# Row sums on ScalarE, other buffer bases, a reordered beginning, and a small matmul ahead of one product in each step

## What is computed

```
h   = x @ W0 + b0
x1  = layernorm(x + (adj @ h) / rowsum(adj))
u   = relu(adj @ (x1 @ W1) + b1)
u   = relu(adj @ (u  @ W2) + b2)
out = layernorm(x1 + adj @ (u @ W3) + b3)
```

## Time and profile before

| | us |
|---|---|
| median of 3 runs (lowest, highest) | 559.99 (559.52, 560.68) |
| the profiled execution | 559.2 |
| its span, first to last instruction | 557.3 |
| PE busy in the span | 545.2 (98%) |
| DVE, ACT, POOL busy | 352.3, 275.1, 207.3 |

### The profile page before, as it was taken

How to read it: one execution, slowest core, us unless ns; L and a number is a source line. 1 busy time by engine, 2 the same in 40 slices (tenths; PEclk the granted TensorE clock), 3 DMA queues, 4 the chain that set the end, 5 groups by cost and what they waited for, 6 DMA issues and landing times.

```text
span 557.3 us, 10510 instructions
## 1 busy us (share of the span) xinstructions
PE 545.2 (98%) x3664; PEld 499.7 (90%) x3664; DVE 352.3 (63%) x1075; ACT 275.1 (49%) x645; POOL 207.3 (37%) x224
## 2 busy tenths in 40 slices
PE   8899999999999999999999999999999999999996
PEld 8788989989899898989989899898989989899885
DVE  5764665747567475665747667475665756657455
ACT  5465454463644536454464644636454364543632
POOL 2647226081450906317071350905318072361000
PEclk9999999999999999999999999999999999999999
DMA  6900230503105050140503205040140502200002
GB/s 229 307 13 1 57 135 1 188 2 110 80 0 188 0 180 9 48 140 0 188 0 99 89 0 188 0 169 19 38 151 0 188 1 71 119 1 39 2 1 76
DMA packets 13270, 43.55 MB, mean 78 GB/s; under 512 B 1728, under 2 KB 2496, under 8 KB 13248
## 3 DMA queue, kind: packets, MB, share of 16 engines
q1 hardware_dynamic: 12960, 42.74, 22.4%
q10 hardware_dynamic: 288, 0.52, 0.3%
HBM read 34.87 MB, written 8.39 MB: 78 GB/s over the span
## 4 chain that ended last, share of the span: by engine, by line
PE 94%; issue 2%; DVE 2%; ACT 1%; DMA 1%; POOL 0%; POOLq 0%; DVEq 0%; SPq 0%
PE bank_a L157 16%; PE bank_a L159 16%; PE bank_a L158 16%; PE bank_b L157 15%; PE bank_b L158 15%; PE bank_b L159 15%; DMA adj_raw<-in_adjT 1%; DVE x_lo L555 0%; DVE x L604 0%; DVE v L597 0%; DVE h_lo L555 0%; POOL adj_lo L748 0%; ACT x_hi L459 0%; ACT adj_hi L396 0%; ACT bank_a L461 0%
## 5 line engine op out<-in xcount | busy, mean ns | idle before, releaser
L748 POOL TENSOR_TENSOR adj_lo<-adj_raw,adj_hi 128x512 fp32r<-128x512 f32 x61 | 77.0, 1295 | 288.3 <-ACT adj_hi L396 288.3
L555 DVE TENSOR_TENSOR x_lo<-bank_a,x_hi 128x512 fp32r<-128x512 f32 x64 | 44.3, 692 | 68.7 <-ACT bank_a L461 68.7
L157 PE MATMUL bank_b<-h_hi,adj_hi 128*128 128x258 f32 x256 | 72.4, 283 | 2.2 <-DVE h_lo L555 2.2
L158 PE MATMUL bank_b<-h_lo,adj_hi 128*128 128x258 f32 x256 | 72.3, 282 | 0.0
L159 PE MATMUL bank_b<-h_hi,adj_lo 128*128 128x258 f32 x256 | 72.2, 282 | 0.0
L157 PE MATMUL bank_b<-s_hi,adj_hi 128*128 128x256 f32 x256 | 70.9, 277 | 0.9 <-DVE s_lo L555 0.9
L159 PE MATMUL bank_b<-s_hi,adj_lo 128*128 128x256 f32 x256 | 70.7, 276 | 0.0
L158 PE MATMUL bank_b<-s_lo,adj_hi 128*128 128x256 f32 x256 | 70.7, 276 | 0.0
L436 ACT ACTIVATE std<-moments,eps_col 128x1 f32<-128x1 f32 x64 | 18.9, 295 | 93.3 <-DVE moments L616 93.3
L479 ACT ACTIVATE std<-moments,eps_col 128x1 f32<-128x1 f32 x64 | 18.9, 295 | 80.1 <-DVE moments L656 80.1
L459 ACT ACTIVATE x_hi<-bank_a,b_col 128x512 fp32r<-128x512 f32 x64 | 43.8, 684 | 21.9 <-PE bank_a L159 20.7
(11 more groups left out here) (84 smaller groups left out, 1586.4 us busy)
## 6 DMA issues: line engine op xcount, KB each, us to landing
adj_raw<-in_adjT SPq DMA_DIRECT2D x32, 512.0 KB, 5.4
x_raw<-in_x SPq DMA_DIRECT2D x16, 512.0 KB, 7.4
xT_raw<-in_xT SPq DMA_DIRECT2D x15, 512.0 KB, 6.6
out_y<-y SPq DMA_DIRECT2D x15, 512.0 KB, 2.9
w_raw<-in_w SPq DMA_DIRECT2D x3, 256.0 KB, 4.3
...
```

The costliest lines, as they stand in the source:

```text
L157: pe.matmul(acc, st[0], mv[0], start=start, stop=False)
L158: pe.matmul(acc, st[0], mv[1], start=False, stop=False)
L555: return dve.tensor_tensor(lo, full, hi.bitcast(F32), ALU.subtract)
L748: pool.tensor_tensor(adj_lo[:, s, k, :], adj_raw[:, k, :], adj_hi[:, s, k, :].bitcast(F32), ALU.subtract).then_inc(done, 1)
```

## The change

1. **Row sums.** `adj` is also loaded in its natural layout into a new buffer `adj_rows` (one more transfer of 1 MB per batch on SP's queue, waiting for `rows_ready`). In ScalarE's `norm2` a new `row_sum` follows each square root: a copy of 128 x 512 in place, whose accumulated output is the row sum. `norm1` takes one reciprocal of four row sums per batch. p1 has 256 columns in place of 258. The first two batches keep the column of ones.
2. **Bases.** `adj`, `x1` and `s2` now follow `w`, then two small buffers (32 bytes each) shift the rest. Modulo 128 bytes, `w`, `adj`, `x1` and `s2` start at 0, and `xT`, `g`, `x2`, `x3`, `s3`, `h` and `zeros` at 64. The rows of `h` are 288 elements (1152 bytes) apart.
3. **Beginning.** All loads come from SP's queue, w0 first. The first p0 (`p0_first`) starts without the low parts, and takes both hi by hi products first. adj of the second batch goes into `adj_rows`, so its load doesn't wait. VectorE splits all of the first adj, behind h. WARM is 18 in place of 16.
4. **The small matmul.** Each p6 has a matmul of zeros ahead of its first product, 128 columns wide, into the bank that this product then overwrites.

```diff
+H_ROW = 288
-WARM = 16
+WARM = 18
...
+        adj_rows = sb("adj_rows", [P, T, N], F32)
...
         w_hi, w_lo = pair("w", [P, 4, KF, F])
+        adj_hi, adj_lo = pair("adj", [P, RING, T, N])
+        x1_hi, x1_lo = pair("x1", [P, T, F])
+        s2_hi, s2_lo = pair("s2", [P, T, F])
+        inv_rows = sb("inv_rows", [P, T], F32)
+        std1 = sb("std1", [P, T], F32)
         xT_hi, xT_lo = pair("xT", [P, T, KF, P])
-        adj_hi, adj_lo = pair("adj", [P, RING, T, N])
-        h_hi, h_lo = pair("h", [P, T, F + ONES])
-        x1_hi, x1_lo = pair("x1", [P, T, F])
         g_hi, g_lo = pair("g", [P, KF, N])
         x2_hi, x2_lo = pair("x2", [P, KF, N])
-        s2_hi, s2_lo = pair("s2", [P, T, F])
         x3_hi, x3_lo = pair("x3", [P, KF, N])
         s3_hi, s3_lo = pair("s3", [P, T, F])
+        h_hi, h_lo = pair("h", [P, T, H_ROW])
...
+            sp.dma_start(w_raw[:, 0, :, :], w0).then_inc(w_loaded[0], DMA)
...
             sp.wait_ge(xT_split, 2)
             sp.dma_start(xT_raw[:, :], xT[1]).then_inc(xT_loaded, DMA)
-            sp.wait_ge(adj_split, T)
-            sp.wait_ge(adj0_last_split, 1)
-            sp.dma_start(adj_raw[:, first_half, :], adjT[1, :, first_half, :]).then_inc(adj_loaded[0], DMA)
-            sp.dma_start(adj_raw[:, second_half, :], adjT[1, :, second_half, :]).then_inc(adj_loaded[1], DMA)
+            for half, tiles in enumerate(halves):
+                sp.dma_start(adj1_raw[:, tiles, :], adjT[1, :, tiles, :]).then_inc(adj1_loaded[half], DMA)
...
                 sp.dma_start(x_raw[:, :, :], x[i]).then_inc(x_loaded, DMA)
+                sp.wait_ge(rows_ready, i * T)
+                sp.dma_start(adj_rows[:, :, :], adj[i]).then_inc(rows_loaded, DMA)
...
+            def p0_first():
+                for j in range(T):
+                    half = j // (T // 2)
+                    pe.wait_ge(xT_hi_ready, half + 1)
+                    for k in range(KF):
+                        pe.matmul(bank_b[j][:, 0:F], xT_hi[:, j, k, :], w_hi[:, 0, k, :], start=k == 0, stop=False)
+                    pe.wait_ge(w0_split, 1)
...
+                width = F + ONES if new is second else F
...
             def p6(old, reader, read):
+                def ready(j):
+                    pe.wait_ge(reader, at(read, T, j + 1))
+                    if j == 0:
+                        pe.matmul(bank_b[0][:, 0:P], zeros[:, 0:P], zeros[:, 0:P], start=True, stop=True)
                 pe.wait_ge(x3_split, at(old, KF, KF))
-                xw_product(p6_done, bank_b, (columns(x3_hi), columns(x3_lo)), 3,
-                           lambda j: pe.wait_ge(reader, at(read, T, j + 1)))
+                xw_product(p6_done, bank_b, (columns(x3_hi), columns(x3_lo)), 3, ready)
...
+            def row_sum(nxt, j):
+                if j == 0:
+                    act.wait_ge(rows_loaded, at(nxt, DMA, -DMA))
+                act.activation(adj_rows[:, j, :], adj_rows[:, j, :], ACT.Copy,
+                               accum_out=rows[:, j:j + 1]).then_inc(rows_ready, 1)
...
-            act.dma_start(w_raw[:, 0, :, :], w0).then_inc(w_loaded[0], DMA)
-            act.dma_start(xT_raw[:, half], xT[0, :, half]).then_inc(xT0_loaded[1], DMA)
...
+                    if a == 0 and not from_columns:
+                        dve.wait_ge(rows_ready, at(new, T, T))
+                        dve.reciprocal(inv_rows[:, :], rows[:, :]).then_inc(inv_rows_ready, 1)
```

More of the change, by code:

```diff
@@ L15, with build @@
 ONES = 2
-WARM = 16
-def build(nc, xT, x, adjT, w0, w1, w2, w3, b0, b1, b2, b3, out):
+H_ROW = 288
+WARM = 18
+def build(nc, xT, x, adjT, adj, w0, w1, w2, w3, b0, b1, b2, b3, out):
     NB = x.shape[0]
@@ L67, in build @@
         y = sb("y", [P, T, F], F32)
-        inv_rows = sb("inv_rows", [P, T], F32)
+        rows = sb("rows", [P, T], F32)
         stats1 = sb("stats1", [P, T, 6], F32)
@@ L88, in build @@
         adj_loaded = [sem(f"adj_half{n}_loaded") for n in range(2)]
+        adj1_loaded = [sem(f"adj1_half{n}_loaded") for n in range(2)]
+        rows_loaded = sem("rows_loaded")
+        rows_ready = sem("rows_ready")
+        inv_rows_ready = sem("inv_rows_ready")
         stored = sem("stored")
@@ L168, in half_of @@
                 return slice(half * n // 2, (half + 1) * n // 2)
-            first_half, second_half = half_of(0, T), half_of(1, T)
-            sp.dma_start(xT_raw[:, first_half], xT[0, :, first_half]).then_inc(xT0_loaded[0], DMA)
-            sp.dma_start(adj_raw[:, first_half, :], adjT[0, :, first_half, :]).then_inc(adj_loaded[0], DMA)
-            sp.dma_start(adj_raw[:, second_half, :], adjT[0, :, second_half, :]).then_inc(adj_loaded[1], DMA)
+            sp.sem_inc(rows_ready, 2 * T)
+            halves = [half_of(half, T) for half in range(2)]
+            sp.dma_start(w_raw[:, 0, :, :], w0).then_inc(w_loaded[0], DMA)
+            for half, tiles in enumerate(halves):
+                sp.dma_start(xT_raw[:, tiles], xT[0, :, tiles]).then_inc(xT0_loaded[half], DMA)
+            for half, tiles in enumerate(halves):
+                sp.dma_start(adj_raw[:, tiles, :], adjT[0, :, tiles, :]).then_inc(adj_loaded[half], DMA)
             sp.dma_start(x_raw[:, :, :], x[0]).then_inc(x_loaded, DMA)
@@ L246, in warm_up @@
                     pe.matmul(bank_a[T - 1][:, 0:F], zeros[:, 0:P], zeros[:, :], start=True, stop=True)
+            def p0_first():
[5 more added lines that the diff above has]
+                    pe.wait_ge(w0_split, 1)
+                    for k in range(KF):
+                        pe.matmul(bank_b[j][:, 0:F], xT_hi[:, j, k, :], w_lo[:, 0, k, :], start=False, stop=False)
+                    pe.wait_ge(xT_split, half + 1)
+                    for k in range(KF):
+                        mm = pe.matmul(bank_b[j][:, 0:F], xT_lo[:, j, k, :], w_hi[:, 0, k, :],
+                                       start=False, stop=k == KF - 1)
+                    mm.then_inc(p0_done, 1)
             def p1_first(tiles):
@@ L522, in _ @@
             h(second, bank_a)
-            norm1(FIRST, None, range(2, T + 1))
+            norm1(FIRST, None, range(2, 3))
             split_w(1)
+            norm1(FIRST, None, range(3, T + 1))
             norm1(second, None, range(0, 1))
@@ L742, in split_w, with split_adj @@
                                    ALU.subtract).then_inc(w_split, 1)
-            def split_adj(nxt, done, tiles=range(T)):
+            def split_adj(nxt):
                 s = slot(nxt)
-                for k in tiles:
+                raw = adj1_raw if nxt is second else adj_raw
+                for k in range(T):
                     pool.wait_ge(adj_hi_ready, at(nxt, T, k + 1))
-                    pool.tensor_tensor(adj_lo[:, s, k, :], adj_raw[:, k, :], adj_hi[:, s, k, :].bitcast(F32),
-                                       ALU.subtract).then_inc(done, 1)
+                    pool.tensor_tensor(adj_lo[:, s, k, :], raw[:, k, :], adj_hi[:, s, k, :].bitcast(F32),
+                                       ALU.subtract).then_inc(adj_split, 1)
             def split_xT(nxt):
@@ L765, in step @@
                 add_b3(new)
-            split_adj(FIRST, adj0_last_split, range(T - 1, T))
             pool.wait_ge(b_loaded[0], DMA)
@@ L771, in _ @@
             pool.wait_ge(adj_split, T)
-            split_adj(second, adj_split)
+            split_adj(second)
             add_b0(second)
@@ L803 @@
         "adjT": adj.reshape(NB, P, T, P, T).transpose(0, 3, 4, 2, 1).reshape(NB, P, T, N),
+        "adj": adj.reshape(NB, P, T, N),
     }
```

62 lines of the change are left out of this document (35 added, 27 removed).

## The result

| | us |
|---|---|
| changed kernel, median of 4 (lowest, highest) | 556.54 (556.17, 556.88) |
| kernel before, beside it, median of 4 | 560.25 (559.52, 560.68) |
| ratio, 95% interval | 0.9939 (0.9927 to 0.9951) |
| the profiled execution, its span | 556.21, 554.4 |

The direction is the predicted one, and the time lies inside the range, but the gain is about half of the 7.1 us.

What follows compares the result with a forecast made beforehand. TensorE was taken to bound the kernel, by matmul count and spacing. Terms -1.4 (p1), -0.6 (p0), -4.9 (p5, p2), +1.8 (small matmul), 0 (row sums), -2.0 (beginning) sum to -7.1 us: forecast 552.9, range 544 to 561.

Steps and rivals of the forecast that it cites:

- the beginning: Start of the kernel: p0 starts near 5.3 us, first p2 moves to 21.6; 2.0 us less, ends 0.8 and 3.5.
- p5 and p2, -4.9: 512-column stages with x1 and s2 at 0: 226.7 ns per matmul instead of 233.3, 4.9 us less.
- p1, -1.4: p1 with 256 columns and h at 64: 5.66 us instead of 5.76 in 14 steps, 1.4 us less.
- My rule of what turns the pace: Between stages: pace changes where one's last moving buffer and the next's stationary buffer share a base; gave p1 5.66 us.
- p0, -0.6, and p4: p0 with xT at 64 takes p4's 2.83 us, 0.6 us less over 14 steps; p4 stays at 2.83.
- The small matmul, +1.8: Zeros ahead of p6: 113 ns each in 16 p6, 1.8 us more, with p6 and p7 keeping their pace.
- rival 5: At p6 and p7: the small matmul holds no pace, both fall to 117.9 ns; 557.6 us, chance 0.08.
- Row sums, 0: ScalarE's four row-sum copies per step are hidden by p4 with 1.3 us to spare, costing 0.
- Rival 1: All 256-column stages run fast: p1 -4.5, p0 -2.1, p4 -1.5, giving 546.8 us; chance 0.20.
- Rivals 2 and 4: At p5 and p2, equal bases do nothing (233.3 ns, 557.8 us, chance 0.10) or slow them (240.0 ns, 562.8 us, 0.09).
- Rival 3: Buffer bases do nothing in any stage, p1 gains only its two columns: 559.2 us, chance 0.08.

Runs made afterwards that it cites:

- e3: Changed kernel with W0 and the second half of x transposed issued from ScalarE's queue, the first half first on SyncE's; 553.08 us.
- e9: Changed kernel with W0 alone issued from ScalarE's queue, both halves of x transposed from SyncE's; 553.85 us.
- e2: Changed kernel with the whole beginning of the kernel before put back; 554.33 us.
- e8: e3 with two small buffers moved ahead of x1, so x1 and s2 start at 64 modulo 128 bytes again; 559.60 us.
- e15: e3 with p1 multiplying all 258 columns of h in every step; 555.77 us.
- e11: e3 with a second small matmul of zeros, ahead of p0, its moving zeros at 0 modulo 128 bytes; 551.55 us.
- e13: e11 with the rows of h 1280 bytes apart instead of 1152; 549.87 us.
- e1: Changed kernel without the small matmul of zeros ahead of p6; 556.58 us.

## Why the prediction was wrong in size

**The step that failed is the beginning.** I took 2.0 us less, from "The start is near 5.3, 0.9 us sooner" to "I move it by 2.0 us, to 21.6"; it came out 2.35 later, 4.35 off, and that alone turns -7.1 into -2.75, where the profiled execution is 3.0 shorter than before. The start at 5.3 held (5.34), for the first half of xT_hi was ready at 5.20 as in the old trace (5.18). The next words, "I expect its end 0.9 to 1.3 sooner", did not: the first p1 ended at 17.77, 1.0 later than before. I asked of no load behind that first half when it would land, although the diff moves two loads off ScalarE's queue and puts W0 ahead of x transposed on SyncE's. I priced the waits that the new loads no longer have, and not the queue on which they now all stand. Taking W0 and the second half off this queue gives 3.5 us back (e3), taking W0 alone off it 2.2 to 2.7 (e9).

Even with two queues the step was too large. What the rest of the new beginning is worth is e3 against e2: 553.08 against 554.33, 1.25 us less, inside my ends of 0.8 to 3.5 but short of 2.0 (each run of e3 is shorter than each of e2, though their first p5 are at 41.28 and 41.43). The first p1 takes 6.69 us there where it took 5.74, for VectorE's splits of adj, and ends 0.5 sooner, not 0.9. GpSimd's split of the second adj, which I put near 19, ends at 20.37 (22.70 in the changed kernel), and the second h_lo, which I put near 19.2, at 20.97 (23.32). In e3 x1_lo of the first batch came 1.0 us sooner than in e2 (22.20 against 23.22), which starts p2; the two last x1_lo, 1.83 us for both beside GpSimd's additions, ended at the same 28.1 in both profiles. VectorE, and not adj, set the pace by then.

**p5 and p2, -4.9.** Right: 226.7 ns to the digit, and e8 shows the cause. The digit was luck: I took the middle of two ends 26.7 ns apart. e8's run lost 6.5 us and not 4.9. Its fourteen steps account for 5.3, as every second one is 0.1 us longer than p5 and p2 explain; the rest lies in the choice of executions, for the two profiled ones are 4.6 apart and the medians 6.5.

**p1, -1.4.** Right in size (5.65 for 5.66) and wrong in its reason. I gave the 6.7 ns between p1 and p7 to the bases, and 0.8 ns to the two columns. e15 shows otherwise: the columns cost 2.5 ns, the base nothing at 258 columns. The 4.4 ns that are left come from the slow pace behind p4 and, in the fast one, from rows of 1152 bytes (e11 and e13). My rule of what turns the pace, equal bases of the last moving and the next stationary buffer, fails here: p4 to p1 has them (w and adj, 0 and 0), but p1 is slow behind a slow p4 and fast behind a fast one (5.44 us in e13). Rows 4 don't bear it out either, since p4 at 117.9 and the p7 behind it at 118.3 are the same pace.

**p0, -0.6, and p4.** Right (2.83 each), and so was what I leaned on, that the pace turns from s3 to xT. e1 and e8 show the turn in the other direction. (p0 took 119.6 ns before; the 120.0 in later lines is rounded up.)

**The small matmul, +1.8.** Its own cost was right: zeros and p6 take 2.84 us, p6 alone 2.73 at the fast pace. But I took p6 as fast without it. With x1 at 0 it isn't (e1), so rival 5 had the wrong state as its start, and the net effect is about 0. So the steady terms as a sum came out (-5.1, and -5.25 for steps and end by the profiled spans), but p1's reason and what the small matmul does were wrong.

**Row sums, 0.** Right; ScalarE's fourth one has 0.19 us more for its ACTIVATION_READ_ACCUMULATOR, and the cover is 1.44 us.

**The rivals.** Rival 1 needed more than the change does: e13 is that case (549.87; it adds a second small matmul, the rows of 1280 bytes and the two queues). Rivals 2 and 4 fell with 226.7 ns. Rival 3, the rule of the Trainium skill's SBUF — State Buffer ("Who interferes with whom"), would leave e8 equal to e3; it is 1.1% slower (0.9989 against 0.9877), so here the measurement stands against it. None of the rivals was about the beginning, and the range for it began above 0.
